# Edge attribute sums by sender: from a product over all blocks to pre-summed rows added in DRAM

## The chip, the cores and the metric

The kernel runs on one core of one Trainium2 chip. The metric is device time in microseconds (us) of one execution. Of the kernel before there are three runs, 2778.34, 2779.93 and 2783.31 us (median 2779.93), and one profiled execution.

## The reference

A graph of 3125 nodes (128 features) and 50000 edges, sorted by receiver `dst`, goes through four layers: a mean aggregation repeated three times, an MLP on edge means, an attention layer (GATv2) and a convolution with radial weights. What matters here is the second layer's input and the first layer beside which it is made:

```
# layer 1, three times: every node adds the mean of its senders' rows
neigh = segment_sum(h[src], dst) / max(deg, 1);  h = h + neigh
# layer 2: means of the 16 edge attributes, by sender and by receiver
rec_attr  = segment_sum(edge_attr_16, src) / max(count(src), 1)
sent_attr = segment_sum(edge_attr_16, dst) / max(count(dst), 1)
h = leaky_relu(concat([x, rec_attr, sent_attr]) @ W1 + b1) @ W2 + b2
```

The receivers are sorted, so edges of one receiver lie together. The senders are random.

## The kernel before

Nodes are padded to 3200, 25 blocks (NBLK) of 128. Edges come in 391 tiles of 128. A visit is a pair of a tile and a block of receivers that it touches: there are 415 visits (NV), taken in 83 batches (NB) of five (VB). An edge of a tile belongs to just one visit; in the others it counts as invalid.

After a setup (ids and attributes are gathered, turned by PE transposes and copied into the tiles EI and AT, the fills of L574 and L829), the adjacency matrix is built in PSUM and stored in DRAM (L849, L1307, L583, L391). Then comes the stage that the change touches.

**The aggregation stage.** It has 75 steps: three layers of 25 blocks of receivers. In a step PE multiplies the block's row of the adjacency (1.6 MB, 3200 columns by 128 partitions) with H, 25 f32 products that the profile counts as 50 (L1335). Three such rows fit into SBUF (RING = 3); SP fetches the row of step n from DRAM when step n-3 is done (L396, L397), 66 fetches in all. DVE scales the sums and adds them (`update_block`, L886 to L898).

Beside a step, one batch of edge attributes is summed; eight steps of the second layer have two (`BATCH_OF`, L196). DVE prepares a batch (`attr_batch`, L861):

- For the sums by receiver: one-hot rows OHD in bf16 (five compares, L881) and the attributes cut into three bf16 parts (L870, L875, L879, L883, L884), whose products are exact enough. PE multiplies 128x48 per visit into the block of receivers that a register names (L1322).
- For the sums by sender: since a sender can be in any of the 25 blocks, DVE makes the one-hot of the block (L871), the one-hot of the row in the block in f32 (`one_hot`, L836), and `products`, the attributes and a one (SA = 17 columns) times the block's one-hot, 25 x 17 = 425 columns per visit (L876). PE multiplies 128x425 in f32 into one bank, where all sums by sender grow (L1319).

DVE runs one step ahead: it prepares the batches of step n+1, then updates the block of step n. `attr_batch(k)` waits until PE has summed batch k-2 (L865), since buffers alternate. PE waits for `attrs_hot` (L1317) and, ahead of a step, for the block updated two steps before (L1332).

GpSimd (POOL) does nothing in this stage. In later stages it issues indirect DMAs, which gather 128 rows by a list of indices: L518 in the attention's scores, L535 in the convolution. After the stage DVE divides both sums (L909 to L916, to `means_ready`), PE turns the means, and the MLP follows.

Of the kernel before, what the change touches and what calls it, by code (L numbers as in the profile page):

```python
# [19 lines left out]
P = 128  # L20
# [6 lines left out]
VB = 5  # L27
# [38 lines left out]
SA = 17  # L66
# [9 lines left out]
def gnn_program(nc, x, edge_ids, last_dst, edge_attrs, species, w1a, w1b, b1, w2, row_params, wlr, wup,  # L76
                wr1, wr2, wdn_a, wdn_b, wsk, out):
    ctx = ExitStack()
    with ctx:
# [14 lines left out]
        radial_hidden = dram("radial_hidden", [VPG * RG * 8, P])  # L94
        dst_in_block = dram("dst_in_block", [VG * P * P], mybir.dt.int16)
# [11 lines left out]
        EI = sb("EI", [P, 5, VW])  # L107
# [115 lines left out]
        FILLS = [(g, j) for g in range(VG) for j in range(2)] + [(g, j) for g in range(VG) for j in range(2, 9)]  # L223
        N_FILL = len(FILLS)
        ACT_FILLS = 18
# [9 lines left out]
        def fill_copy(f):  # L235

            g, j = FILLS[f]
            n = 1 if j == 1 else 4
            if j < 2:
                w = P  # L240
                dst = view(EI, 4 * j * VW + g * P, [[VW, n], [1, w]])
            else:
                w = min(P, NV + 1 - g * P)
                row = (0, 4, 8, 12, SH, RAD, RAD + 4)[j - 2]
# [4 lines left out]
        def OHS(p):  # L249

            return view(OH, p * VB * P, [[P, VB], [1, P]])

        def products(p):

            return view(SCR, p * VB * NBLK * SA, [[NBLK * SA, VB], [SA, NBLK], [1, SA]])

        OHD_AT = 0
        PARTS3_AT = OHD_AT + 2 * VB * P // 2
        SBH_AT = PARTS3_AT + 2 * VB * 24
        LEFT_AT = SBH_AT + 2 * VB * NBLK  # L260
        assert LEFT_AT + 2 * VB * 16 <= DEPTH * VB * D
# [5 lines left out]
        def attr_parts(p):  # L267

            return view(G, PARTS3_AT + p * VB * 24, [[1, VB * 24]]).bitcast(BF16).rearrange("p (v n) -> p v n", v=VB)


# [22 lines left out]
        BACK = 5  # L294
# [78 lines left out]
        def _(sp):  # L373
# [6 lines left out]
            sp.dma_start(block_of_visit, vrow[:, 0:P]).then_inc(s("blocks_out"), 16)  # L380
            sp.wait_ge(s("blocks_out"), 16)
            sp.dma_start(rowi[:, 2 * NT:2 * NT + VW], block_of_visit.rearrange("g v -> (g v)").rearrange("(o n) -> o n", o=1)).then_inc(s("blocks_in"), 16)
            for g in range(VG):
                sp.wait_ge(s("kinds_ready"), g + 1)
                sp.dma_start(dst_in_block[g * P * P:(g + 1) * P * P].rearrange("(p n) -> p n", p=P),
                             view(RX, 20 * P + g * P // 2, [[1, P // 2]]).bitcast(mybir.dt.int16)).then_inc(s("near_stored"), 16)
                sp.wait_ge(s(f"attrs_in{g % 2}"), 16 * (g // 2 + 1))
                sp.dma_start(radial_rows[g * P:(g + 1) * P, :], view(SCR, (g % 2) * N_ATTR * P + 20 * P, [[1, 8 * P]])).then_inc(s(f"radial_rows_stored{g % 2}"), 16)
# [3 lines left out]
            for r in range(RING):  # L392
                sp.wait_ge(s(f"block_moved{r}"), 16 * len(range(r, NBLK, RING)))
            for n, (i, b, slot, fetch) in enumerate(STEPS):
                if fetch:
                    sp.wait_ge(s("block_summed"), n - RING + 1)  # L396
                    sp.dma_start(view(RX, slot * ABLK, [[1, ABLK]]), adjacency[b]).then_inc(s(f"block_moved{slot}"), 16)  # L397
            for i in range(2):
# [5 lines left out]
                if i == 0:  # L404
# [6 lines left out]
                    sp.wait_ge(s("radial_zeroed"), 1)  # L411
                    for j in range(VPG):
                        sp.dma_start(wr1_s[8 * j:8 * j + 8, 8 * j:8 * j + 8], wr1.rearrange("(a q) c -> a q c", q=VB)[:, 0, 0:8]).then_inc(s("radial_loaded"), 16)
                    for k in range(NB + DEPTH):
                        if k < NB:
                            if k >= DEPTH:
                                sp.wait_ge(s("z_hot"), k - DEPTH + 1)
                            sp.dma_start(near(k % DEPTH), dst_in_block[k * VB * P:(k + 1) * VB * P].partition_broadcast(P)).then_inc(s(f"near_in{k % DEPTH}"), 16)
                        if k >= DEPTH:
                            i, m = (k - DEPTH) % ROWS_RING, (k - DEPTH) // ROWS_RING  # L420
                            sp.wait_ge(s(f"score_gathered{i}"), 16 * VB * (m + 1))
                            sp.dma_start(gathered_rows[k - DEPTH], score_rows(i).rearrange("p a b -> p (a b)")).then_inc(s(f"rows_stored{i}"), 16)
# [31 lines left out]
        def _(pool):  # L454
# [23 lines left out]
            for g in range(VG):  # L478
                at = bass.IndirectOffsetOnAxis(ap=tvi[:, g:g + 1], axis=0)
                if g >= 2:  # L480
                    pool.wait_ge(s("fill_turned"), 2 * VG + 7 * (g - 1))
# [26 lines left out]
            pool.memset(wr1_s[:], 0.0).then_inc(s("radial_zeroed"), 1)  # L508
            pool.wait_ge(s("idx_made"), 1)
            pool.wait_ge(s("table_written"), written(1))  # L510
            for k in range(NB):
                i, m = k % ROWS_RING, k // ROWS_RING
                if k >= ROWS_RING:
                    pool.wait_ge(s("z_read"), k - ROWS_RING + 1)
                    pool.wait_ge(s(f"rows_stored{i}"), 16 * m)
# [26 lines left out]
        def _(act):  # L542
# [33 lines left out]
            act.wait_ge(s("near_stored"), 16 * VG)  # L576
# [55 lines left out]
            def weights_and_hot(k, p):  # L632
# [7 lines left out]
                for q in range(VB):  # L640
                    ins = act.activation(OH[:, p, q, :], iota[:], ACT.Abs, bias=view(EI, 3 * VW + VB * k + q, [[1, 1]]), scale=-1.0)
# [25 lines left out]
        def _(dve):  # L667
# [88 lines left out]
            dve.wait_ge(s("blocks_in"), 16)  # L756
# [41 lines left out]
            for g in range(VG):  # L798
# [4 lines left out]
                st = [view(RX, (5 * g + i) * P, [[1, P]]) for i in range(5)]  # L803
# [3 lines left out]
                done(dve.tensor_scalar(st[3], dr[:, 1], tv[:, 5, g:g + 1], None, ALU.add))  # L807
                va, vb, vc = (view(HT, 1792 + 128 * i, [[1, P]]) for i in range(3))
                dve.tensor_copy(view(RX, 20 * P + g * P // 2, [[1, P // 2]]).bitcast(mybir.dt.int16), st[3])
                dve.tensor_copy(st[2], view(HT, 1664, [[1, P]]).bitcast(I32))  # L810
                dve.tensor_copy(vc, view(HT, 1536, [[1, P]]).bitcast(I32))
                done(dve.tensor_scalar(va, st[3], 0.0, None, ALU.is_ge))
                done(dve.scalar_tensor_tensor(vb, st[3], float(P - 1), va, ALU.is_le, ALU.mult))

                done(dve.scalar_tensor_tensor(vc, vb, -64.0, vc, ALU.mult, ALU.add))
                dve.tensor_scalar(st[1], vc, 64.0, None, ALU.add)
                dve.tensor_scalar(invalid_neg[:, g, :], vb, 1.0, BIG, ALU.subtract, ALU.mult)
                done(dve.tensor_tensor(va, dr[:, 1], dr[:, 2], ALU.not_equal))
                dve.tensor_tensor(st[4], va, vb, ALU.mult).then_inc(s("kinds_ready"), 1)
# [3 lines left out]
            dve.wait_ge(s("fill_copied_act"), 2 * VG)  # L823
# [8 lines left out]
            dve.wait_ge(s("ones_made"), 2)  # L832
# [6 lines left out]
            dve.wait_ge(s("key_iota_made"), 2)  # L839
# [17 lines left out]
            dve.memset(PS[:, 2, :], 0.0)  # L857
            dve.memset(PS[:, 4:8, :], 0.0).then_inc(s("sums_zeroed"), 1)
            dve.wait_ge(s("visit_built"), NVA)

            def attr_batch(k):  # L861
# [4 lines left out]
                attrs = lambda n: view(AT, VB * k, [[1, VB], [NV + 1, n]])  # L866
                part = lambda j: attr_parts(p)[:, :, j * 16:(j + 1) * 16]
                left = view(G, LEFT_AT + p * VB * 16, [[16, VB], [1, 16]])
                sbh = lambda dims: view(G, SBH_AT + p * VB * NBLK, dims)
                dve.tensor_copy(part(0), attrs(16))  # L870
# [4 lines left out]
                split = mark(dve.tensor_tensor(left, attrs(16), part(0), ALU.subtract))  # L875
# [4 lines left out]
                for q in range(VB):  # L880
                    dve.tensor_scalar(OHD(p)[:, q], iota_h[:, KEYS:KEYS + P], view(EI, 3 * VW + VB * k + q, [[1, 1]]), None, ALU.is_equal)  # L881
                dve.wait_ge(s("dve_step"), split)
                done(dve.tensor_tensor(left, left, part(1), ALU.subtract))  # L883
                dve.tensor_copy(part(2), left).then_inc(s("attrs_hot"), 1)  # L884

# [15 lines left out]
            for n in range(LAYERS * NBLK):  # L901
# [3 lines left out]
                update_block(n)  # L905
            dve.wait_ge(s("attrs_summed"), NB)
            by_src = view(PS, 2 * 512, [[SA, NBLK], [1, SA]])
            by_dst = view(PS, 4 * 512, [[DSLOT, NBLK], [16, 3], [1, 16]])
            done(dve.tensor_scalar(small[:, 0, :], by_src[:, :, 16], 1.0, None, ALU.max))  # L909
            done(dve.reciprocal(inv_deg[:, 0, :], small[:, 0, :]))  # L910
            dve.tensor_copy(means[:, :, 0:16], by_src[:, :, 0:16])
            done(dve.tensor_copy(means[:, :, 16:32], by_dst[:, :, 0, :]))
            done(dve.tensor_tensor(means[:, :, 16:32], means[:, :, 16:32], by_dst[:, :, 1, :], ALU.add))
# [108 lines left out]
            for i in range(DEPTH, ROWS_RING):  # L1022
                dve.wait_ge(s(f"rows_stored{i}"), 16 * len(range(i, NB, ROWS_RING)))
# [539 lines left out]
```

## Time and profile before

| | |
|---|---|
| median of three runs | 2779.93 us |
| profiled execution | 2787.6 us |
| its span | 2785.8 us |
| PE busy | 2016.9 us (72%) |
| DVE busy | 2019.5 us (72%) |
| ACT busy | 499.4 us (18%) |
| POOL busy | 896.0 us (32%) |
| share of the chain that ended last | PE 40%, POOL 23%, DVE 21%, issue 12% |
| costliest lines of that chain | PE L1335 14%, PE L1319 9%, POOL L518 9% and 6%, POOL L535 8% |

The span is the profiled execution from its first to its last instruction; 1.8 us lie around it. Busy shares are means over stages with different limits: PE and DVE have the same 72%, and which of the two sets the pace must be read stage by stage. A matmul's duration in a group's mean is longer than the distance to the next one, since matmuls are pipelined.

### The profile page before, as it was taken

The numbers are of one execution on the slowest core, as the hardware profiler recorded it, in microseconds if no ns is written. First come the engines' busy times: TensorE is split into PE (matmuls) and PEld (weight loads), VectorE is DVE, ScalarE is ACT, GpSimd is POOL, SyncE is SP. The second block draws the span as 40 slices with busy tenths as digits, with TensorE's granted clock in tenths as the row PEclk, the third lists the DMA queues.
The fourth block names the chain that finished last, engine by engine and source line by source line (L and its number), as shares of the span: only waits on it lengthen the run. The fifth ranks groups of instructions, "written<-read, shape, count | busy, mean of one in ns | idle before, by whom it ended". The sixth has DMA issues, their size and how long they took to land.

```text
span 2785.8 us, 42113 instructions
## 1 busy us (share of the span) xinstructions
PE 2016.9 (72%) x10841; PEld 1503.3 (54%) x10841; DVE 2019.5 (72%) x5209; ACT 499.4 (18%) x1184; POOL 896.0 (32%) x888
## 2 busy tenths in 40 slices
PE   3777777999899999985444334326884778878887
PEld 2322224888678888854333333315773656666666
DVE  8888888778797777767555555578557777777775
ACT  2222221000000000011000000002221444444441
POOL 2000000000000000004777777725000577777770
PEclk9999999999999999997555555556896676777778
DMA  5222223453234344504444444413441222222120
GB/s 182 97 119 95 119 95 142 168 183 123 95 130 178 119 166 166 187 2 138 126 128 125 129 126 124 127 60 114 125 127 30 64 53 53 53 54 53 53 53 27
DMA packets 98876, 300.01 MB, mean 108 GB/s; under 512 B 21520, under 2 KB 48919, under 8 KB 86432
## 3 DMA queue, kind: packets, MB, share of 16 engines
q1 hardware_dynamic: 69566, 232.90, 24.6%
q0 software_dynamic: 27904, 64.15, 8.8%
q8 instruction: 100, 1.64, 0.2%
q10 hardware_dynamic: 1250, 0.86, 0.1%
q14 instruction: 56, 0.46, 0.1%
HBM read 220.86 MB, written 76.97 MB: 107 GB/s over the span
## 4 chain that ended last, share of the span: by engine, by line
PE 40%; POOL 23%; DVE 21%; issue 12%; DMA 2%; ACT 1%; SPq 1%; DVEq 0%; POOLq 0%; ACTq 0%
PE PS L1335 14%; PE PS L1319 9%; POOL G L518 9%; POOL G L535 8%; POOL SCR L518 6%; DVE SCR L849 5%; PE PS L1439 5%; DVE G L848 4%; PE PS L1474 3%; DVE SCR L876 2%; PE PS L1307 1%; PE PS L1462 1%; PE PS L1308 1%; PE PS L1442 1%; PE PS L1309 1%
## 5 line engine op out<-in xcount | busy, mean ns | idle before, releaser
L518 POOL DMA_INDIRECT G<-table,src_idx x255 | 259.7, 1019 | 1296.9 <-DMA table<-RX 1219.5
L535 POOL DMA_INDIRECT G<-table,gather_idx x415 | 415.5, 1001 | 373.7 <-DMA table<-RX 247.5
L1394 PE MATMUL PS<-RX,OH 128*128 x830 | 208.2, 434 | 310.4 <-DVE OH L964 309.7
L1474 PE MATMUL PS<-SCR,OH 128*128 128x256 f32 x830 | 309.8, 544 | 108.7 <-DVE SCR L1204 108.7
L1394 PEld LDWEIGHTS PS<-RX,OH 128*128 128x128 f32 x830 | 183.7, 322 | 338.6 <-issue 337.8
L876 DVE TENSOR_TENSOR SCR<-G,AT 128x2125 f32<-128x2125 f32 x83 | 318.9, 3842 | 0.0
L1319 PE MATMUL PS<-SCR,OH 128*128 128x425 f32 x830 | 312.7, 523 | 3.5 <-DVE G L884 3.2
L1474 PEld LDWEIGHTS PS<-SCR,OH 128*128 128x128 f32 x830 | 218.6, 273 | 168.7 <-DVE RX L1169 110.8
L1335 PE MATMUL PS<-HB,RX 128*128 128x132 f32 (+1 forms) x2500 | 292.5, 277 | 0.6 <-ACT RX L583 0.6
L1335 PEld LDWEIGHTS PS<-HB,RX 128*128 128x128 f32 x2500 | 283.9, 191 | 1.0 <-ACT RX L583 1.0
L849 DVE TENSOR_SCALAR SCR<-iota_h,OH 128x400 bf16<-128x400 int16 x790 | 250.4, 317 | 0.0
L848 DVE TENSOR_SCALAR G<-iota_h,OH 128x128 bf16<-128x128 int16 x790 | 195.9, 248 | 53.5 <-PE PS L1309 48.9
L1307 PE MATMUL PS<-SCR,G 128*128 128x400 bf16 x395 | 142.2, 360 | 103.7 <-DVE SCR L849 73.8
L1319 PEld LDWEIGHTS PS<-SCR,OH 128*128 128x128 f32 x830 | 151.6, 191 | 116.8 <-issue 112.5
L836 DVE TENSOR_TENSOR OH<-iota,EI 128x640 f32<-128x640 f32 x166 | 145.0, 874 | 76.8 <-PE PS L1442 76.7
L1439 PE MATMUL PS<-G,OH 128*128 128x128 f32 x830 | 162.4, 348 | 49.4 <-issue 25.9
L1169 DVE TENSOR_TENSOR RX<-RX,PS 128x256 f32 x415 | 171.1, 412 | 13.9 <-PE PS L1474 2.3
L518 POOL DMA_INDIRECT SCR<-table,src_idx x160 | 160.8, 1005 | 48.7 <-issue 48.7
L1439 PEld LDWEIGHTS PS<-G,OH 128*128 128x128 f32 x830 | 137.0, 223 | 65.0 <-issue 57.2
L1335 PE MATMUL PS<-SCR,RX 128*128 128x128 f32 x1250 | 148.1, 279 | 7.2 <-DVE SCR L896 7.2
L583 ACT COPY RX<-PS 128x400 f32<-128x400 f32 x200 | 98.5, 492 | 284.4 <-PE PS L1309 283.8
L1185 DVE TENSOR_TENSOR SCR<-G,AT 128x480 f32<-128x480 f32 x83 | 54.7, 659 | 130.7 <-DMA G<-table,gather_idx 84.3
(309 smaller groups left out, 2904.6 us busy)
## 6 DMA issues: line engine op xcount, KB each, us to landing
RX<-adjacency SPq DMA_DIRECT2D x66, 1600.0 KB, 6.7
adjacency<-RX SPq DMA_DIRECT2D x25, 1600.0 KB, 6.1
RX<-gathered_rows SPq DMA_DIRECT2D x83, 320.0 KB, 3.0
gathered_rows<-G SPq DMA_DIRECT2D x51, 320.0 KB, 2.4
AT<-dst_in_block SPq DMA_DIRECT2D x83, 160.0 KB, 3.9
gathered_rows<-SCR SPq DMA_DIRECT2D x32, 320.0 KB, 2.4
G<-table,gather_idx POOLq DMA_INDIRECT x415
G<-table,src_idx POOLq DMA_INDIRECT x255, 2.7
```

Of the source, the lines that this page charges most:

```text
L518: pool.indirect_dma_start(score_rows(i)[:, q], None, tables[0], bass.IndirectOffsetOnAxis(ap=src_idx[:, v:v + 1], axis=0)).then_inc(s(f"sc ...
L535: pool.indirect_dma_start(G[:, p, q, :], None, tables[i], bass.IndirectOffsetOnAxis(ap=gather_idx[:, p, q:q + 1], axis=0)).then_inc(s(f"{n ...
L848: dve.tensor_scalar(src_hot(v, j), iota_h[:, KEYS:KEYS + P], KS[:, 2 + j, v:v + 1], None, ALU.is_equal)
L849: ins = dve.tensor_scalar(key_hot(v, j), iota_h[:, 0:KEYS], KS[:, j, v:v + 1], None, ALU.is_equal)
L876: dve.tensor_tensor(products(p), sbh([[NBLK, VB], [1, NBLK], [0, SA]]), view(AT, VB * k, [[1, VB], [0, NBLK], [NV + 1, SA]]), ALU.mult)
L1169: dve.tensor_tensor(acc, acc, PS[:, q, 0:MSG], ALU.add).then_inc(s("added"), 1)
L1307: pe.matmul(PSF[:, bass.ds(bank, KEYS)], src_hot(v, 0), key_hot(v, 0), start=False, stop=False, skip_group_check=True)
L1319: pe.matmul(PS[:, 2, 0:NBLK * SA], OHS(p)[:, q], products(p)[:, q], start=False, stop=False, skip_group_check=True)
L1335: ins = pe.matmul(PS[:, n % 2, 0:w], adj(slot)[:, c], H_OF[i][:, c, 0:w], start=c == 0, stop=c == NBLK - 1)
L1394: ins = pe.matmul(view(PS, k % DEPTH * 1024 + 171 * q, [[1, XR_W]]), view(OH, (k % DEPTH * VB + q) * P, [[1, P]]), view(RX, b * XR_W, [[1, ...
L1439: pe.matmul(PSF[:, bass.ds(b * P, P)], OH[:, p, q, :], G[:, p, q, :], start=False, stop=False, skip_group_check=True)
L1474: ins = pe.matmul(PS[:, q, 0:MSG], OH[:, p, q, :], view(SCR, M_AT + (p * VB + q) * MSG, [[1, MSG]]), start=True, stop=True)
```

## The change

Sums by sender are no longer made by one product over all blocks. For each visit PE multiplies a 128x128 matrix of 0 and 1, which says which edges of the tile have the same sender, with the attributes in bf16 parts. Every edge then holds the sum over its twins, the edges of the visit with its sender. The first of each set of twins is found, and its row of 49 values (three parts of 16 and the count) is added to the sender's row of a DRAM table by an indirect DMA that accumulates. There are five tables, one for each place q of a visit in its batch; an add to a table waits until the table's last add has landed. The other edges send their rows to 128 spare rows.

- Setup: 24 fills instead of 36 (the radial attributes' rows and one kind are no longer turned). The sender's key is stored to DRAM too as int16 rows (`sender_of_visit`). SP clears the five tables (five DMAs of 3328 x 49 values).
- `attr_batch`: L871, L836 and L876 go. Five compares (`twin_hot`) between the keys of all 128 edges in a row, fetched by SP as a broadcast DMA of 160 KB per batch (`row16_in`), and the edge's own key come.
- PE: five bf16 products of 128x51 (48 attribute parts, a one, and two columns that mark whether an earlier edge has the same sender) take the place of L1319.
- `place`, new on DVE after `update_block`: it copies the five sums from PSUM, compares the two marks with limits made of the partition number, and writes the row to which each edge's sum goes.
- POOL: 83 x 5 indirect DMAs that add.
- After the last step SP reads the five tables back, DVE adds them, and the means use the three parts.

```diff
 def attr_batch(k):
...
-    split = mark(dve.tensor_tensor(sbh([[NBLK, VB], [1, NBLK]]), view(iota, 0, [[0, VB], [1, NBLK]]),
-                                   view(EI, VW + VB * k, [[1, VB], [0, NBLK]]), ALU.is_equal))
-    one_hot(OHS(p), 2, k)
+    dve.wait_ge(s(f"row16_in{k % DEPTH}"), 16 * (k // DEPTH + 1))
+    for q in range(VB):
+        dve.tensor_scalar(twin_hot(p)[:, q], sender(k % DEPTH)[:, q * P:(q + 1) * P], EI[:, 1, VB * k + q:VB * k + q + 1], None, ALU.is_equal)
...
-    dve.tensor_tensor(products(p), sbh([[NBLK, VB], [1, NBLK], [0, SA]]),
-                      view(AT, VB * k, [[1, VB], [0, NBLK], [NV + 1, SA]]), ALU.mult)
...
+def place(k):
+    sums = twin_sums(k % DEPTH)
+    both = view(begins, FLAG_AT, [[2, VB], [1, 2]])
+    first = view(begins, FLAG_AT + 2 * VB, [[1, VB]])
+    dve.wait_ge(s("twins_summed"), k + 1)
+    if k >= DEPTH:
+        for q in range(TABLES):
+            dve.wait_ge(s(f"scattered{q}"), 16 * (k - DEPTH + 1))
+    dve.tensor_copy(sums, view(PS, (2 + k % 2) * 512, [[TWIN_W, VB], [1, TWIN_W]])).then_inc(s("twins_copied"), 1)
+    dve.wait_ge(s("twins_copied"), k + 1)
+    done(dve.tensor_tensor(both, sums[:, :, SENT_W:TWIN_W], limits, ALU.is_lt))
+    done(dve.tensor_tensor(first, both[:, :, 0], both[:, :, 1], ALU.mult))
+    done(dve.tensor_tensor(first, first, key_shift[:, VB * k:VB * (k + 1)], ALU.mult))
+    dve.tensor_scalar(sent_to[k % DEPTH], first, dummy, None, ALU.add).then_inc(s("sent_placed"), 1)
...
 # PE, attr_sums(k)
+    if k >= 2:
+        pe.wait_ge(s("twins_copied"), k - 1)
     for q in range(VB):
-        pe.matmul(PS[:, 2, 0:NBLK * SA], OHS(p)[:, q], products(p)[:, q], start=False, stop=False, skip_group_check=True)
+        ins = pe.matmul(PS[:, 2 + p, q * TWIN_W:(q + 1) * TWIN_W], twin_hot(p)[:, q], attr_parts(p)[:, q, 0:TWIN_W], start=True, stop=True)
+    ins.then_inc(s("twins_summed"), 1)
...
 # POOL
+pool.wait_ge(s("sent_cleared"), 16 * TABLES)
+for k in range(NB):
+    pool.wait_ge(s("sent_placed"), k + 1)
+    for q in range(VB):
+        if k >= 1:
+            pool.wait_ge(s(f"scattered{q}"), 16 * k)
+        pool.indirect_dma_start(sent_sums[q], bass.IndirectOffsetOnAxis(ap=sent_to[k % DEPTH][:, q:q + 1], axis=0),
+                                twin_sums(k % DEPTH)[:, q, 0:SENT_W], None, compute_op=ALU.add).then_inc(s(f"scattered{q}"), 16)
...
 # SP, in the loop over steps, and after it
+    for k in BATCH_OF[n]:
+        if k >= DEPTH:
+            sp.wait_ge(s("attrs_hot"), k - DEPTH + 1)
+        sp.dma_start(sender(k % DEPTH), sender_of_visit[k * VB * P:(k + 1) * VB * P].partition_broadcast(P)).then_inc(s(f"row16_in{k % DEPTH}"), 16)
...
+sp.wait_ge(s("block_summed"), LAYERS * NBLK)
+for q in range(TABLES):
+    sp.wait_ge(s(f"scattered{q}"), 16 * NB)
+    sp.dma_start(sent(q), sent_sums[q][0:NPAD, :].rearrange("(p n) d -> p (n d)", p=P)).then_inc(s("sent_in"), 16)
...
 # DVE, ahead of the means
+dve.wait_ge(s("sent_in"), 16 * TABLES)
+for q in range(1, TABLES):
+    done(dve.tensor_tensor(sent(0), sent(0), sent(q), ALU.add))
```

## Rows read from the trace of the kernel before

**Rows 1.** Busy time in 500:600 us: busy us (count) by engine; clock, DMA share, GB/s
```profile
500.00:600.00 100.00, 100.00 (x688) 80.74 (x687) 78.18 (x193) 0.00 (x0) 0.00 (x0) 1.00 0.51 181
```

**Rows 2.** Groups in 460:1211 us: line, engine, operation; busy us, mean ns; idle, releaser
```profile
L1319 PE MATMUL PS<-SCR,OH 128*128 128x425 f32 x830 | 312.7, 523 | 3.5 <-DVE G L884 3.2
...
L876 DVE TENSOR_TENSOR SCR<-G,AT 128x2125 f32<-128x2125 f32 x83 | 318.9, 3842 | 0.0
...
L836 DVE TENSOR_TENSOR OH<-iota,EI 128x640 f32<-128x640 f32 x83 | 67.9, 818 | 0.0
...
L881 DVE TENSOR_SCALAR G<-iota_h,EI 128x128 bf16<-128x128 int16 x415 | 74.7, 252 | 0.0
...
L870 DVE CAST G<-AT 128x80 bf16<-128x80 f32 x83 | 19.6, 236 | 142.8 <-PE PS L1322 142.8
```

**Rows 3.** One step in order of time: start us, length us, engine, line, operation, count
```profile
503.12 5.87 PE L1335 MATMUL PS<-HB,RX 128*128 128x132 f32 x50
...
503.31 0.24 DVE L870 CAST G<-AT 128x80 bf16<-128x80 f32 x1 [1.82 <-PE PS L1322]
...
508.83 3.74 PE L1319 MATMUL PS<-SCR,OH 128*128 128x425 f32 x10
...
509.74 0.15 DVE L892 TENSOR_SCALAR small<-PS 128x1 f32<-128x1 f32 x1
...
510.57 0.29 DVE L898 SCALAR_TENSOR_TENSOR X<-SCR,X 128x128 f32<-128x128 f32 x1
...
512.40 0.29 PE L1322 MATMUL PS<-G 128*128 128x48 bf16 x5
...
512.53 5.87 PE L1335 MATMUL PS<-HB,RX 128*128 128x132 f32 x50
```

**Rows 4.** The stage's first matmuls, its first wide product, and its end, in order of time
```profile
460.32 5.89 PE L1335 MATMUL PS<-HB,RX 128*128 128x132 f32 x50 [0.58 <-ACT RX L583]
...
469.39 5.53 PE L1319 MATMUL PS<-SCR,OH 128*128 128x425 f32 x10 [3.18 <-DVE G L884]
...
1210.63 0.18 DVE L909 TENSOR_SCALAR small<-PS 128x25 f32<-128x25 f32 x1 [3.02 <-PE PS L1322]
...
1214.11 0.57 DVE L916 TENSOR_TENSOR means<-means,inv_deg 128x400 f32<-128x400 f32 x1
```

**Rows 5.** Groups of the whole span: a PSUM read and a long add on DVE
```profile
L1169 DVE TENSOR_TENSOR RX<-RX,PS 128x256 f32 x415 | 171.1, 412 | 13.9 <-PE PS L1474 2.3 <-DVE RX L1169 0.7
...
L952 DVE TENSOR_TENSOR HB<-RX 128x3200 f32<-128x3200 f32 x1 | 3.5, 3493 | 0.2 <-ACT RX L601 0.2
```

**Rows 6.** Gathers on POOL and a compare on DVE, in order of time
```profile
1398.71 0.95 POOL L518 DMA_INDIRECT G<-table,src_idx  x1 [0.30 <-issue]
...
1398.96 0.54 DVE L964 TENSOR_SCALAR OH<-AT,tv 128x640 f32<-128x640 int16 x1
...
1405.20 0.96 POOL L518 DMA_INDIRECT G<-table,src_idx  x1 [0.30 <-issue]
```

**Rows 7.** Busy time in 2250:2350 us, columns as in Rows 1
```profile
2250.00:2350.00 100.00, 82.70 (x315) 63.52 (x314) 74.25 (x185) 46.40 (x122) 76.57 (x77) 0.73 0.20 53
```

**Rows 8.** DMA issues: KB each, us to landing; last, queue in 500:600 us: packets, MB, share
```profile
RX<-adjacency SPq DMA_DIRECT2D x66, 1600.0 KB, 6.7
...
AT<-dst_in_block SPq DMA_DIRECT2D x83, 160.0 KB, 3.9
...
SCR<-table,src_idx POOLq DMA_INDIRECT x160, 2.7
...
radial_rows<-SCR SPq DMA_DIRECT2D x4, 512.0 KB, 2.7
...
SCR<-in_edge_attrs,tvi POOLq DMA_INDIRECT x4, 9.4
...
q1 hardware_dynamic: 1584, 18.02, 50.5%
```

**Rows 9.** One operation of the setup's loop over groups, in order of time
```profile
43.57 0.29 DVE L815 SCALAR_TENSOR_TENSOR RX<-RX 128x128 f32<-128x128 f32 x1
```

More of the change, by code:

```diff
@@ L94, in gnn_program @@
         radial_hidden = dram("radial_hidden", [VPG * RG * 8, P])
+        sender_of_visit = dram("sender_of_visit", [VG * P * P], mybir.dt.int16)
+        sent_sums = [dram(f"sent_sums{q}", [NPAD + P, SENT_W]) for q in range(TABLES)]
         dst_in_block = dram("dst_in_block", [VG * P * P], mybir.dt.int16)
@@ L237, in fill_copy, with sender, twin_hot, twin_sums @@
             g, j = FILLS[f]
-            n = 1 if j == 1 else 4
-            if j < 2:
+            n = 4
+            if j == 0:
                 w = P
-                dst = view(EI, 4 * j * VW + g * P, [[VW, n], [1, w]])
+                dst = view(EI, g * P, [[VW, n], [1, w]])
             else:
                 w = min(P, NV + 1 - g * P)
-                row = (0, 4, 8, 12, SH, RAD, RAD + 4)[j - 2]
+                row = (0, 4, 8, 12, SH)[j - 1]
                 dst = view(AT, row * (NV + 1) + g * P, [[NV + 1, n], [1, w]])
             return dst, view(PS, (2 + f % 6) * 512, [[P, n], [1, w]])
[L249 to L255, printed above, removed]
         OHD_AT = 0
[L258 to L261, printed above, removed]
+        EQ_AT = DEPTH * VB * P // 2
+        TWINS_AT = EQ_AT + 2 * VB * P // 2
+        LEFT_AT = TWINS_AT + 2 * VB * 26
+        FLAG_AT = LEFT_AT + 2 * VB * 16
+        assert FLAG_AT + 3 * VB <= 4 * NT + 600
+        SUMS_AT = RAD * (NV + 1)
+        SENT_AT = SUMS_AT + DEPTH * VB * TWIN_W
+        SHIFT_AT = SENT_AT + DEPTH * VB
+        LIMIT_AT = SHIFT_AT + NV + 1
+        assert LIMIT_AT + 16 <= ROWS * (NV + 1) and VB * TWIN_W <= 512
+        ZERO_AT = ROWS * (NV + 1) - (NBLK + 1) * SENT_W
+        assert LIMIT_AT + 16 <= ZERO_AT
+        def sender(i):
+            return view(begins, i * VB * P // 2, [[1, VB * P // 2]]).bitcast(mybir.dt.int16)
+        def twin_hot(p):
+            return view(begins, EQ_AT + p * VB * P // 2, [[1, VB * P // 2]]).bitcast(BF16).rearrange("p (v n) -> p v n", v=VB)
+        def twin_sums(i):
+            return view(AT, SUMS_AT + i * VB * TWIN_W, [[TWIN_W, VB], [1, TWIN_W]])
+        sent_to = [view(AT, SENT_AT + i * VB, [[1, VB]]).bitcast(I32) for i in range(DEPTH)]
+        key_shift = view(AT, SHIFT_AT, [[1, NV]])
+        limits = view(AT, LIMIT_AT, [[0, VB], [1, 2]])
+        marks = view(AT, LIMIT_AT + 2, [[0, VB], [1, 3]])
+        dummy = view(AT, LIMIT_AT + 5, [[1, 1]])
         def OHD(p):
@@ L806, in _ @@
                 dve.tensor_scalar(view(HT, 1664, [[1, P]]).bitcast(I32), idr[:, 0:P], 127, None, ALU.bitwise_and)
[L807 to L810, printed above, removed]
+                done(dve.tensor_scalar(st[2], dr[:, 1], tv[:, 5, g:g + 1], None, ALU.add))
@@ L811, in _ @@
+                va, vb, vc, vd = (view(HT, 1792 + 128 * i, [[1, P]]) for i in range(4))
+                row16 = lambda at: view(RX, at + g * P // 2, [[1, P // 2]]).bitcast(mybir.dt.int16)
+                dve.tensor_copy(row16(20 * P), st[2])
+                dve.tensor_copy(vd, view(HT, 1664, [[1, P]]).bitcast(I32))
                 dve.tensor_copy(vc, view(HT, 1536, [[1, P]]).bitcast(I32))
-                done(dve.tensor_scalar(va, st[3], 0.0, None, ALU.is_ge))
-                done(dve.scalar_tensor_tensor(vb, st[3], float(P - 1), va, ALU.is_le, ALU.mult))
@@ L815, in _ @@
-                done(dve.scalar_tensor_tensor(vc, vb, -64.0, vc, ALU.mult, ALU.add))
-                dve.tensor_scalar(st[1], vc, 64.0, None, ALU.add)
+                done(dve.tensor_scalar(va, st[2], 0.0, None, ALU.is_ge))
+                done(dve.scalar_tensor_tensor(vb, st[2], float(P - 1), va, ALU.is_le, ALU.mult))
                 dve.tensor_scalar(invalid_neg[:, g, :], vb, 1.0, BIG, ALU.subtract, ALU.mult)
+                done(dve.scalar_tensor_tensor(vc, vd, float(NBLK), vc, ALU.mult, ALU.add))
@@ L818, in _ @@
+                done(dve.scalar_tensor_tensor(vc, iota[:], -1.0, vc, ALU.mult, ALU.add))
+                done(dve.scalar_tensor_tensor(vc, vc, -float(NPAD), vb, ALU.add, ALU.mult))
+                done(dve.scalar_tensor_tensor(st[1], vc, float(NPAD), iota[:], ALU.add, ALU.add))
+                dve.tensor_copy(row16(22 * P), st[1])
                 done(dve.tensor_tensor(va, dr[:, 1], dr[:, 2], ALU.not_equal))
-                dve.tensor_tensor(st[4], va, vb, ALU.mult).then_inc(s("kinds_ready"), 1)
+                dve.tensor_tensor(st[3], va, vb, ALU.mult).then_inc(s("kinds_ready"), 1)
```

139 lines of the change are left out of this document (84 added, 55 removed).

## The prediction

> **What bounds the kernel now.** I read the page first: its table of engines and its costliest groups name two lines of the aggregation stage, L1319 and L876. Then the busy time by stretches. In 500 to 600 us TensorE (PE) is busy 100.00 of 100 us at granted clock 1.00 (2.4 GHz), VectorE (DVE) 78, GpSimd (POOL) none, and the DMA engines 0.51 of the time [rows 1]. The reader is to see that one engine has no slack, one has a fifth, and one sleeps. The groups of the stage say what PE and DVE do: the wide product of L1319 takes 312.7 us of PE, L876 prepares it in 318.9 us of DVE, and DVE's only large wait, 142.8 us at L870, is for PE [rows 2]. Last the order of one step: 50 adjacency matmuls start at 503.12, the wide product at 508.83, the short product L1322 at 512.40, the next step's at 512.53. A period is 9.41 us: 5.71 + 3.57 + 0.13 [rows 3]. The stage runs from 460.32 to the means at 1214.68 (1214.11 + 0.57), 754.4 us [rows 4]. It is PE's, step after step.
>
> **What goes.** PE's 3.57 us per batch. On DVE: L876, 3.84 us per batch, L836 at 0.82 and the little L871. A batch of DVE work now spans 503.31 to 509.74, 6.43 us, of which the three hold about 4.7 (3.84 + 0.82; L871 overlaps mostly), so some 1.8 stay.
>
> **What comes on PE.** Five bf16 products of 51 columns per batch. The nearest row is L1322, five of 48 columns in 0.29 us. So PE needs 5.71 + 0.13 + 0.29 = 6.13 us for a step with one batch. The wait on twins_copied is for the batch two back, done long before.
>
> **What comes on DVE.** Five compares for the twins, like L881's (five take 0.9 us: 74.7 us for 83 batches [rows 2]): a batch is 2.7 us. The block update is 1.12 us at most (509.74 to 510.57 + 0.29). place() copies 128x255 from PSUM, nearest L1169 with 0.41 [rows 5], and has four tiny operations that wait on each other; such a one takes some 0.2 with its wait in the update's chain: 1.3 in all. Sum 2.7 + 1.1 + 1.3 = 5.1 us, under 6.13. In the eight steps with two batches it is 8.7 at the lower update cost, above PE's 6.6. Wait added: place() waits for this step's twin product, and behind it stands the next attr_batch; the product follows block_summed by 0.3 us while the update runs, so it costs nothing as long as PE is not late. It also waits for the scatters of batch k-3, which matters only if POOL lags.
>
> **What comes on POOL.** This sets the end, I think. There are 5 x 83 = 415 indirect DMAs that add rows in DRAM, on an engine that is idle here. The trace has no scatter and no add. The nearest rows are POOL's gathers of 128 rows: 0.95 us busy, and five of them with their gaps take 1398.71 to 1405.20 = 6.49 us, 1.30 each [rows 6]. Another stage runs at the same pace, 77 in 100 us [rows 7]. 6.49 per batch is already above PE's 6.13 and DVE's 5.1: POOL becomes the bound, and in steps with two batches (13.0) even more; POOL falls back there until place() holds DVE, DVE holds PE. So the stage is 83 times POOL's pace, x.
>
> What could x be? Lower end: 0.96 each, without the 0.30 between (issue gaps stand ahead of all gathers, so I don't believe it); then PE and DVE bind: 67 x 6.13 + 8 x 8.7 = 480 us. Nearest row: 6.49. Upper end: POOL may not add to table q before the add of the batch before has landed. A gather lands 2.7 us after issue, one of 14 KB rows 9.4 [rows 8]. If each add took 9.4 and the round did not start earlier, x would be about 10. Between them are the DMA engines. In 500 to 600 us ten fetches and a bit moved 18.02 MB in 1584 packets, 11.4 KB each, at 50.5% of the engines' time [rows 8]: 4.8 us a fetch. A scatter gives each of 16 engines eight rows, and a row may have to wait for such a packet, about 0.5 us (50.5 us x 16 / 1584). Eight times that on 2.7 is 6.8 us, just over the 6.49 after which POOL comes back to the same table, and a stall results only in rounds that meet a fetch. I take x = 7.0: the row plus 0.5 for an add that is dearer than a gather and for these stalls. It is nearer to 6.49 than to 10 because everything measured of POOL's small indirect DMAs is in the low row.
>
> On the same point the Trainium skill, "SBUF — State Buffer", section "SBUF: two separate sides", speaks against the change: while VectorE runs an instruction in a mode with two ports, GpSimd cannot write descriptors and waits for the end. Each batch would have ten compares on DVE. Whether it holds is seen at L964, a tensor_scalar from int16 of 128x640 in 0.54 us, shorter than L836 of the same size (0.82): it began 0.25 us into a gather, and the gather still took 0.95 [rows 2, 6]. The trace does not bear the rule out here, though that is one kind of compare with a float output. Its price is a rival below.
>
> **The other ends.** Lead: the first batch was ready at 469.39 [rows 4]. DVE now has some 3 us of constants ahead and 3.8 us less in the batch, then batch 1 (2.7), update and place: first scatter about 474, so 13.7 us after 460.3. Tail, all exposed, since PE and DVE have nothing else: the last add lands 1.4 after its issue ends (2.7 less about 1.3), the last table of 612 KB comes in 3.0 (512 KB took 2.7 [rows 8]), four dependent adds of 1225 columns at 3.49 / 3200 us a column [rows 5] are 5.7 with gaps, the means chain 4.1 as now and one more operation 0.6: 14.8 us. Setup: three more dependent operations of 0.33 (0.29 like L815 [rows 9], and its wait) and a copy in each of four groups, against 12 fewer fills and one transposed kind less: +2 us, between -3 and +5. The five clears (3.1 MB) lie in the setup beside DVE's work; each scatter table waits for them, 400 us later. Sender rows, 160 KB each: such a DMA lands in 3.9 us [rows 8], issued two steps ahead, 13 us. Fetches land in 6.7, also with two steps' lead: at a step of 7 they stay hidden; doubled they would not. SP's order is no trouble: sender k waits only for attrs_hot of k-3.
>
> **Sum.** After: 13.7 + 83 x + 14.8 + 2 = 30.5 + 83 x, against 754.4. With x = 7.0: 611.5, a gain of 142.9. The profiled execution took 2787.6 us (its span 2785.8, 1.8 around it), so 2644.7 by its scale; the median of the runs is 2779.93, 7.7 below, so **2637 us**. Other stages are left as they are: their instructions don't change, and what is queued behind the scatters on POOL, the score gathers of L518, waits for a table that is written only after the MLP.
>
> **The rivals.**
> - Cheap scatters: PE and DVE bind. 9 + 480 + 1.3 + 5 + 14.8 + 2 = 512: 2538 us. For it: nothing but the 0.96 of busy time; against it the 0.30 ahead of each gather. Chance 0.05.
> - The DMA engines are the bound. Per batch 4.8 (fetch) + 0.6 (sender row, estimate: a tenth of a fetch's bytes in shorter rows) + scatters. A gather costs an engine 0.20 x 100 / 77 = 0.26 us [rows 7]; an add must read twice and write: twice that, five times, is 2.6. Sum 8.0, x = 8.0: 694.5, gain 59.9, 2720 us. For it: shares of one engine set do add up. Against: nine of 75 steps have no fetch, and the fetch's 4.8 was taken with nobody else there. Chance 0.17. A fall of PE's clock belongs here: at 0.73, as in [rows 7], 5.71 becomes 7.8 and a step 8.2, 75 of them 618 us: 2675, inside the forecast's own range. That row, where PE is busy 83 of 100 us, speaks for such a fall, since PE would be busy 6.1 of 7.0 us here.
> - DVE's compares lock POOL out: ten at 0.165 is 1.65 a batch, x = 8.14: 706, 2731 us. Against it stands L964. Chance 0.08. (The rule is the one of the page named above.)
> - Slower than before: POOL's wait for its own table. If an add needs 10 us from issue to semaphore, each of the five tables admits one add per 10 us: x = 10, 860.5 us, 106 more than now, 2886 us. It decides from x = (754.4 - 30.5) / 83 = 8.72. For it: the reads and writes in DRAM beside 1.6 MB fetches and the 9.4 us row. Against: 2.7 us for every small gather, among 320 KB stores. Chance 0.14.
> - No change: PE's product is gone but the pace of scatters falls on 8.65 to 8.79. Chance 0.03.
>
> **Numbers.** The forecast (x from 6.49 to 7.8, that is 2595 to 2703) has 0.53. Faster by over 0.2%, which is what a measurement of this kernel can tell: 0.53 + 0.05 + 0.17 + 0.08 = 0.83; within: 0.03; slower: 0.14. The range leaves out the slower case and the cheapest: 2580 to 2755.
>
> **What would show it.** Right: in the profile after, POOL is busy over 70% from about 474 to 1055 and its gaps at the scatter name mostly issue; PE waits for DVE, DVE for POOL's scatters, in the steps after the first double ones; PE's product is 0.29 us; the tail from last scatter to means is 15 us. Wrong: POOL idle before each scatter for the DMA of its table (latency), a scatter busy for clearly more than 0.96 us (descriptors or DVE's lock), fetches landing after 13 us (DMA engines), or a granted clock under 0.9 in the stage.

## The result: 3% slower, and the profile after

The changed kernel takes 2865.98 us (median of four runs, 2863.96 to 2870.28) against 2781.6 us of the kernel before beside it: ratio 1.0305, interval 1.0289 to 1.0321. The forecast was 2637 us. The profiled execution has a span of 2862.8 us, 77.0 more than before.

The busy times by stretch come first, as in [rows 1] (window; PE, weight load, DVE, ACT, POOL busy; granted clock, DMA share, GB/s):

```profile
500.00:600.00 100.00, 77.47 (x673) 73.93 (x671) 47.10 (x254) 0.00 (x0) 78.08 (x52) 0.89 0.86 216
600.00:700.00 100.00, 72.39 (x587) 68.89 (x585) 50.86 (x272) 0.00 (x0) 80.74 (x52) 0.80 0.69 148
700.00:800.00 100.00, 59.56 (x434) 53.51 (x432) 45.27 (x242) 0.00 (x0) 83.15 (x54) 0.73 0.57 110
```

PE had 100 of 100 us at clock 1.00 and now idles; DVE fell from 78 to 47; POOL, idle before, is the busiest. But it does only 52 to 54 scatters in 100 us, where the gathers of [rows 7] came to 77. The line of the scatter says why (durations in ns, minimum / median / maximum; then what POOL waited for, in us and times; then who waited for it):

```profile
L554 POOL DMA_INDIRECT sent_sums<-AT x415: 1552/1553/1804, 478.7 to 1278.8; - x139
its engine sat idle before it (us, times) until:
  DVE AT L968: 411.6, 1
  issue: 110.4, 361
  DMA sent_sums<-AT: 45.6, 53
who waited for it (us, times):
  DVE AT L963: 398.3, 62
```

An indirect DMA that adds keeps POOL busy for 1.55 us; a gather took 0.95 [rows 6]. The 411.6 us are the time before the first one. From 478.7 to the end of the last at 1280.4 there are 801.7 us: 645.7 busy, 110.4 of the gap ahead of each, 45.6 of waits for a table's DMA. That is 9.66 us a batch (7.78 + 1.33 + 0.55). DVE waits 398 us for scatters in place(), and PE waits for DVE behind it. One step in order of time, the rows that answer to [rows 3]:

```profile
883.88 5.82 PE L1427 MATMUL PS<-SCR,RX 128*128 128x128 f32 x50
884.43 1.55 POOL L554 DMA_INDIRECT sent_sums<-AT  x1 [0.30 <-issue]
886.29 1.55 POOL L554 DMA_INDIRECT sent_sums<-AT  x1 [0.30 <-issue]
...
890.00 1.55 POOL L554 DMA_INDIRECT sent_sums<-AT  x1 [0.30 <-issue]
...
891.73 0.43 DVE L963 COPY AT<-PS 128x255 f32<-128x255 f32 x1 [9.06 <-DMA sent_sums<-AT]
...
895.60 0.40 PE L1410 MATMUL PS<-begins 128*128 128x51 bf16 x5 [5.89 <-DVE begins L952]
...
895.82 1.55 PE L1414 MATMUL PS<-begins,G 128*128 128x48 bf16 x5
...
897.27 3.11 PE L1427 MATMUL PS<-SCR,RX 128*128 128x128 f32 x13
```

The adjacency matmuls take 5.8 us as before. Then DVE has waited 9.06 us for the scatters of the batch three back, prepares the next batch late, and PE stands 5.89 us until it is ready. POOL issues every 1.86 us all through this step.

The rest went as the change intended. The groups of the stage answer to [rows 2]: the twin product is cheap, and no DVE group is above 80 us where L876 had 319.

```profile
L1410 PE MATMUL PS<-begins 128*128 128x51 bf16 x415 | 27.5, 199 | 176.0 <-DVE begins L952 124.1 <-DVE AT L963 51.6 <-issue 0.2
```

```profile
L941 DVE TENSOR_SCALAR begins<-begins,EI 128x128 bf16<-128x128 int16 x415 | 78.7, 292 | 4.0 <-DMA begins<-sender_of_visit 4.0
```

The end of the stage, as in [rows 4] (from the last scatter to the means, start and length in us):

```profile
1278.83 1.56 POOL L554 DMA_INDIRECT sent_sums<-AT  x1 [0.30 <-issue]
1289.69 5.85 DVE L995 TENSOR_TENSOR RX<-RX 128x1225 f32<-128x1225 f32 x4 [33.99 <-DMA RX<-sent_sums]
...
1299.54 0.58 DVE L1006 TENSOR_TENSOR means<-means,inv_deg 128x400 f32<-128x400 f32 x1
```

The stage, from the first adjacency matmul (462.0) to the means (1300.1), takes 838.1 us instead of 754.4. It costs 83.7; setup adds 1.7, and 8.4 come back after the means. These 8.4 are not the change's doing: in this execution POOL's 830 gathers are about 0.01 us shorter each (8.9 us in sum), and in the changed kernel's second profile, where they have their old length, what follows the means takes 1570.9 us, as before (1571.1).

### The profile page after: what moved, and what is told of

Its sections match the earlier page's. It is cut to its first block, busy times and chain, and to the rows that moved or that the text cites. A ratio compares the mean times of both kernels' runs of the same rounds, so it can differ in the third digit from the quotient of the medians.

```text
span 2862.8 us, 42728 instructions
## 1 busy us (share of the span) xinstructions
PE 1843.6 (64%) x10390; PEld 1453.3 (51%) x10390; DVE 1802.7 (63%) x5818; ACT 494.8 (17%) x1175; POOL 1533.1 (54%) x1303
## 3 DMA queue, kind: packets, MB, share of 16 engines
q0 software_dynamic: 87664, 74.59, 15.0%
## 4 chain that ended last, share of the span: by engine, by line
POOL 34%; PE 18%; DVE 17%; issue 15%; DMA 14%; ACT 1%; DVEq 0%; POOLq 0%; ACTq 0%
DMA sent_sums<-AT 12%; POOL sent_sums L554 12%; POOL G L565 9%; POOL G L582 7%; POOL SCR L565 6%; PE PS L1531 5%; DVE SCR L900 5%; DVE G L899 4%; PE PS L1566 3%; PE PS L1396 1%; PE PS L1554 1%; PE PS L1397 1%; PE PS L1398 1%; DVE RX L1259 1%; PE PS L1534 1%
## 5 line engine op out<-in xcount | busy, mean ns | idle before, releaser
L554 POOL DMA_INDIRECT sent_sums<-AT x415 | 645.7, 1556 | 567.6 <-DVE AT L968 411.6
L565 POOL DMA_INDIRECT G<-table,src_idx x255 | 257.1, 1008 | 165.0 <-DMA table<-RX 87.6
L1427 PE MATMUL PS<-HB,RX 128*128 128x132 f32 (+1 forms) x2500 | 326.1, 296 | 6.6 <-DVE HB L980 6.0
L1427 PEld LDWEIGHTS PS<-HB,RX 128*128 128x128 f32 x2500 | 317.8, 210 | 7.4 <-DVE HB L980 6.1
L1566 PEld LDWEIGHTS PS<-SCR,OH 128*128 128x128 f32 x830 | 216.7, 271 | 159.9 <-DVE RX L1259 100.4
L963 DVE COPY AT<-PS 128x255 f32<-128x255 f32 x83 | 35.2, 424 | 398.6 <-DMA sent_sums<-AT 398.3
L1259 DVE TENSOR_TENSOR RX<-RX,PS 128x256 f32 x415 | 171.6, 414 | 14.8 <-PE PS L1566 3.6
L1427 PE MATMUL PS<-SCR,RX 128*128 128x128 f32 x1250 | 174.7, 309 | 9.4 <-DVE SCR L980 9.4
L1427 PEld LDWEIGHTS PS<-SCR,RX 128*128 128x128 f32 x1250 | 170.6, 224 | 9.6 <-DVE SCR L980 9.5
L1531 PEld LDWEIGHTS PS<-G,OH 128*128 128x128 f32 x830 | 142.8, 238 | 61.4 <-issue 54.7
L1554 PEld LDWEIGHTS PS<-wr_s,SCR 40*128 40x128 f32 x830 | 128.4, 236 | 48.0 <-issue 48.0
L1554 PE MATMUL PS<-wr_s,SCR 40*128 40x128 f32 x830 | 146.5, 334 | 6.3 <-DMA SCR<-radial_hidden 4.5
```

The costliest lines, as they stand in the source:

```text
L554: pool.indirect_dma_start(sent_sums[q], bass.IndirectOffsetOnAxis(ap=sent_to[k % DEPTH][:, q:q + 1], axis=0), twin_sums(k % DEPTH)[:, q, 0 ...
L565: pool.indirect_dma_start(score_rows(i)[:, q], None, tables[0], bass.IndirectOffsetOnAxis(ap=src_idx[:, v:v + 1], axis=0)).then_inc(s(f"sc ...
L1259: dve.tensor_tensor(acc, acc, PS[:, q, 0:MSG], ALU.add).then_inc(s("added"), 1)
L1427: ins = pe.matmul(PS[:, n % 2, 0:w], adj(slot)[:, c], H_OF[i][:, c, 0:w], start=c == 0, stop=c == NBLK - 1)
L1531: pe.matmul(PSF[:, bass.ds(b * P, P)], OH[:, p, q, :], G[:, p, q, :], start=False, stop=False, skip_group_check=True)
L1554: ins = pe.matmul(view(PS, 5 * 512 + q * P, [[1, P]]), view(SCR, CH_AT + p * P, [[1, P]], 8 * VB), wr2_s[:, q, :], start=True, stop=True)
```

## The experiments

Theory A: the addition is what lengthens POOL's instruction, and 415 of them set the pace. Rivals: B, it is the direction (a scatter, whose indices choose rows in DRAM to be written); C, it is the wait of an add for its own table that sets the pace; D, POOL's time goes by the rows or bytes of an instruction. "Stage" is always from the first adjacency matmul to the means, in the profile. The first run of each of the first four experiments was on one chip, without the changed kernel beside them, so their times are compared with the kernel before alone; the length of an instruction is read from their profiles.

**Writing instead of adding.** On that chip the kernel before took 3031 us; it was run again on another.

```diff
-    twin_sums(k % DEPTH)[:, q, 0:SENT_W], None, compute_op=ALU.add)
+    twin_sums(k % DEPTH)[:, q, 0:SENT_W], None)
```

> The scatters write their rows instead of adding them (the addition is left out, so the tables hold only the last write). Theory A, the addition is what makes POOL's instruction 1.55 us instead of a gather's 0.95: each scatter is busy about 0.95 us, 1.26 with its gap, the pace is 6.3 to 6.5 us a batch, 3.2 us less than the 9.66 measured, and the time falls by 83 x 3.2 = 260 us to about 2600. Theory B, the direction costs (indices on the DRAM side, whatever is done there): 1.55 us stays and the time stays at 2866 within 10 us. Theory C, the wait for the own table sets the pace (landing): busy falls or not, but POOL's idle for the table's DMA takes the place, over 3 us a batch, and the time stays above 2800.

> As the first of its kind (rows written, not added; the sums by sender are wrong for it), for the pace: there POOL's scatter was busy 0.97 us, yet the pace was 8.6 us a batch, with PE starved of instructions (idle before it named issue, 217 us). Theory A, that was the chip: here PE has no such idle and the pace is 6.5 us, time about 2600. Rival, plain scatters starve PE's instruction supply anywhere, or the fetch collides with them: PE idle stays, pace over 8, time over 2730.

First run: 3003.8 us, ratio 0.990 (0.987 to 0.994), with 216.9 us of PE's idle ahead of L1427 named issue, that is, waiting for nothing that the profile shows. Its cause is open; it is absent in the second run, and the pace is read from that one. Second: 2696.16 us, 0.9665 (0.964 to 0.969), stage 657.1 us. The line of the scatter in the second:

```profile
L554 POOL DMA_INDIRECT sent_sums<-AT x415: 963/969/1177, 480.6 to 1099.4; - x139
its engine sat idle before it (us, times) until:
  DVE AT L968: 416.8, 11
  DMA sent_sums<-AT: 114.9, 95
```

In both, 0.97 us instead of 1.55: the addition is what lengthens the instruction, and B falls. The same kernel with nothing but the addition taken out is 6.8 points faster on the ratio than the changed kernel beside it (1.0342, below). What POOL does in the extra 0.58 us no run shows. But the pace is 7.5 us a batch (619.8 / 83: 4.87 busy, 1.17 of gaps, 1.38 for tables), not the 6.5 expected. The rival C has a part: as POOL gets round sooner, it meets tables whose last write hasn't landed, 114.9 us in 95 waits, where it was 45.6 in 53.

**No scatters.** POOL's loop, and the waits for it in place() and on SP, are taken out.

> No scatter is issued at all and nobody waits for one (the sums by sender are left out; tables are cleared and read back as in the changed kernel). It is the floor of PE and DVE. Theory A, POOL's 415 instructions alone set the pace: my sum for PE and DVE, 67 x 6.13 + 8 x 8.7 = 480 us for the steps, so the stage ends at about 462 + 9 + 480 + 13 = 964 instead of 1300, 336 us earlier, time about 2530. Rival, the adjacency fetches (9.0 us to landing in the changed kernel) or the sender rows set a pace of their own at 7.5 to 8 us a step: 2600 to 2640 with PE waiting for DMA. Rival, PE's clock falls as in the changed kernel (0.8) although nothing waits: about 2600.

> No scatters at all (the sums by sender are left out), now beside a kernel before of usual time. The stage alone took 506 us to the means on the other chip; so here 2785 - 754 + 510 = about 2540, with PE at granted clock 1.00 and no idle in it. If the other chip's other stages had hidden something, 2600 or more.

On the first chip 2755.73 us, 0.909 (0.906 to 0.911); on the second 2543.76 us, 0.9115 (0.910 to 0.913), stage 506.1 us:

```profile
500.00:600.00 100.00, 100.00 (x1008) 99.74 (x1007) 76.22 (x417) 0.00 (x0) 0.00 (x0) 1.00 0.84 302
```

PE is full at clock 1.00, with 1008 matmuls in 100 us where it had 688 [rows 1]: 60 a step, so 6.0 us. In the steps with two batches (600 to 700 us) it was 87 of 100. Fetches land in 7.2 us, and PE waits for them 5.6 us in all. The stage was expected at 502 us (9 + 480 + 13), so the floor of PE and DVE is where I had put it, and without scatters the fetches and the clock are no bound of their own. What lies between 506 and 838 us comes with the scatters.

**Half the rows.**

```diff
-    ap=sent_to[k % DEPTH][:, q:q + 1] ... twin_sums(k % DEPTH)[:, q, 0:SENT_W]
+    ap=sent_to[k % DEPTH][0:64, q:q + 1] ... twin_sums(k % DEPTH)[0:64, q, 0:SENT_W]
```

> Each scatter adds 64 rows instead of 128 (the edges in the upper 64 places of each tile are left out of the sums by sender). If POOL's time goes by descriptors, 1.55 us becomes something like 0.9 to 1.1 and the time falls by 415 x 0.5 = about 200 us to 2660. If it is a fixed cost of an adding instruction, 1.55 stays and the time stays at 2866 less the table waits (at most 45 us of idle).

3050.97 us on the slower chip, 1.007 (1.003 to 1.011).

```profile
L554 POOL DMA_INDIRECT sent_sums<-AT x415: 1413/1419/1644, 481.5 to 1244.7; - x139
```

64 rows cost 1.42 us, 128 cost 1.55. By these two, 0.13 us goes with 64 rows; drawn on in a straight line (an estimate), about 1.28 us is left for an instruction without rows. So most of it is paid by instruction.

**Narrow rows.** 17 values instead of 49, in other tables.

```diff
-    pool.indirect_dma_start(sent_sums[q], ... twin_sums(k % DEPTH)[:, q, 0:SENT_W]
+    pool.indirect_dma_start(sent_narrow[q], ... twin_sums(k % DEPTH)[:, q, 0:SEND_W]
```

> Each added row has 17 values (68 B) instead of 49 (196 B), in tables of their own that nobody reads (the sums by sender come out as zero). If bytes count for POOL's 1.55 us or for the DMA engines, the busy time or the waits for the table shrink, and fetches land earlier than 9.0 us: up to 45 us less. If only the number of rows counts, nothing moves: 1.55 us, 2866 within 15 us.

3093.46 us on that chip, 1.020 (1.017 to 1.023); the scatter 1552 ns at the median, the table waits 47.6 us. Bytes count for nothing in POOL's time, and rows for 0.13 us in 64: D falls. The number of packets stayed as it was (87664 in the software queue), so this run doesn't say what fewer packets would do.

**Fewer scatters.** If it is paid by instruction, some visits are better off on PE. The last one, or the last two, of the five visits of a batch go by the old wide product, which needs the sender's block and row again (made from the ids by six DVE operations ahead of the loop), two one-hots and the product on DVE in each batch, and shares PSUM bank 7.

```diff
+WIDE = 2                     # 1 in the other
+TABLES = VB - WIDE
...
+    dve.tensor_tensor(products(p), sbh([[NBLK, WIDE], [1, NBLK], [0, SA]]),
+                      view(AT, VB * k + TABLES, [[1, WIDE], [0, NBLK], [NV + 1, SA]]), ALU.mult)
...
+    for q in range(WIDE):
+        pe.matmul(PS[:, 7, 64:64 + NBLK * SA], OHS(p)[:, q], products(p)[:, q], start=False, stop=False, skip_group_check=True)
```

> The changed kernel itself, beside the others on this chip, since the first four experiments ran on a chip where the kernel before took 3031 us instead of 2780. All theories: 3% over the kernel before on a chip with its usual time; POOL's scatter 1.55 us. If the ratio here is far from 1.03, the ratios of the first four can't be put against it.

> Four of five visits of a batch go by scatter, the fifth by the old wide product (two f32 matmuls of 425 columns, DVE prepares 1 x 425). If POOL's 1.86 us for each scatter is the pace, 4 x 1.86 = 7.44 us a batch plus the table waits 0.4: 83 x 7.8 = 650 + 31 = 681 against 754 of the kernel before: 2705. If it isn't the count of scatters but their latency in the table's chain (one a round, whatever the number), the pace stays at 9.66: 2865.

> Three of five visits by scatter, two by the wide product. POOL: 3 x 1.86 = 5.6 us a batch. PE: 5.84 + 0.13 + 0.17 + 2 x 0.71 = 7.5 us; DVE 5.1 - 0.35 + 2 x 0.97 = 6.7. PE is the bound again: 67 x 7.5 + 8 x 12.5 = 603 + 25 = 628 against 754: about 2655. If the table's chain of latency were the pace: 2865, and if DVE is (with the waits for its own results longer than counted), 2700.

> The same kernel as before with three tables, beside the one with six on the same chip: 0.972 of the kernel before, within 0.003.

The changed kernel again: 2884.03 us, 1.0342 (1.0325 to 1.0359). With four scatters 2801.07, 1.0048 (1.0031 to 1.0065), stage 761.7. With three 2712.5, 0.9717 (0.9701 to 0.9733), and in a second call 2714.22, 0.9721 (0.9703 to 0.9738); stage 673.6. So the time does fall with the count, but one scatter less took the stage from 845.9 us (the changed kernel beside it) to 761.7, 84 us where 157 were expected, and two less fell short too (2655 expected). The line with three scatters shows the table waits, which I had counted at 0.4 us a batch, at 1.7:

```profile
L569 POOL DMA_INDIRECT sent_sums<-AT x249: 1551/1553/3122, 484.1 to 1121.1; - x125
its engine sat idle before it (us, times) until:
  DVE AT L996: 435.9, 24
  DMA sent_sums<-AT: 143.7, 66
...
DMA to landing us min/median/max: 3.1/6.3/10.0
```

This is the only kernel so far whose profile gives the landing of an add: 6.3 us at the median, up to 10.0, against 2.7 of a gather [rows 8]. A round of three scatters would be 5.6 us, less than that, so POOL often meets a table whose last add is under way. The waits for it grow as the rounds shrink: 45.6, 105.0, 143.7 us for five, four, three scatters a batch.

The same line shows a second cost, one that the wide product brings in: the median is still 1553 ns, but the longest add took 3122. The mean is 1711 with three scatters and 1613 with four, against 1556 with five. In order of time:

```profile
505.13 1.62 DVE L970 TENSOR_TENSOR SCR<-G,AT 128x850 f32<-128x850 f32 x1
505.14 3.12 POOL L569 DMA_INDIRECT sent_sums<-AT  x1 [0.30 <-issue]
```

L970 makes `products` from two inputs in SBUF. The add that began 0.01 us after it ended 1.51 us behind the product's end (508.26 and 506.75), about as long as a whole add. In this run 67 of the 249 adds began while L970 ran, and every one ended 1.43 to 1.51 us after the product did, however much of it was left: the add gets on only when the product is over. Over 1.55 us each, that is 36 us of POOL's busy time. How much of it was on the path no run separates.

**Six tables.** Odd and even batches add to different tables.

```diff
+    t = q + k % 2 * TABLES
+    if k >= 2:
+        pool.wait_ge(s(f"scattered{t}"), 16 * (k // 2))
```

> The kernel with three visits by scatter and two by the wide product, but with six tables instead of three: odd and even batches have tables of their own, so an add waits for the one two batches back. There POOL stood idle 143.7 us for a table's DMA, whose landing took 3.1 to 10.0 us (median 6.3). Theory: that idle is on the path in part, PE then sets the pace at about 7.5 us in single steps; less 40 to 60 us, plus 6 to 8 us for three more tables to read and add: 2660 to 2680. Rival: the idle was slack beside PE's pace and nothing is gained, 2715 to 2720. Rival: three adds more in flight delay the adjacency's fetches and one another, slower than 2712.

2677.55 us, 0.9594 (0.9581 to 0.9608), stage about 641 us (639.7 from the first matmul in the profile, which lacks the records of some ahead of it), and the fastest of all that compute the whole result: 4% under the kernel before, 7% under the changed one. It is 36.7 us below the same kernel with three tables beside it, so theory C's share is shown too, at this length of round.

```profile
L570 POOL DMA_INDIRECT sent_sums<-AT x249: 1551/1662/3109, 485.1 to 1079.4; - x125
its engine sat idle before it (us, times) until:
  DVE AT L997: 524.7, 62
  issue: 56.4, 185
  DMA sent_sums<-AT: 0.6, 2
```

The table waits are gone (0.6 us). POOL now waits for DVE (524.7 less the first 416.4). In 500 to 600 us PE was busy 100.00 with three tables already; what the second set gave lies later. The stretch 800 to 900 us, three tables and then six:

```profile
800.00:900.00 100.00, 89.92 (x708) 78.10 (x707) 64.80 (x262) 0.00 (x0) 58.83 (x35) 0.95 0.82 217
800.00:900.00 100.00, 100.00 (x840) 89.18 (x839) 80.92 (x323) 0.00 (x0) 75.59 (x44) 1.00 0.80 206
```

The adds that begin beside the wide product are still long (mean of all 1729 ns).

## Why the prediction was wrong

- **What bounds the kernel before: right.** Without scatters the stage took 506 us; my sum for cheap scatters gave 512, of which 2 are setup and 6.3 the last scatters and their landing, which this run doesn't have. PE 6.0 us a step (6.13 forecast). That floor is also the measure of the gain that there was to take.
- **POOL becomes the bound, DVE waits in place(), PE behind it: right**, and in the order named.
- **The failed step: "I take x = 7.0: the row plus 0.5 for an add that is dearer than a gather and for these stalls".** The row of the gather (6.49) was taken for an instruction that adds. It measured 7.78 + 1.33 + 0.55 = 9.66 (busy, gaps, table waits). The addition in POOL's busy time is 5 x 0.6 = 3.0 us more than five gathers' 4.75; the gaps and waits were 1.88 where 7.0 had left them 2.25, which makes the 2.66 us too few. 83 x 2.66 = 221 of the stage's error of 229 us (838.1 against 13.7 + 581 + 14.8 = 609.5); lead and tail are the other 8. I had the number of instructions, the engine and the chain right, and gave the one operation that no row showed 0.5 us a batch over a gather's row, at most 1.3 at the range's end of 7.8, when nothing but its likeness to a gather held it there.
- **The rivals.** The slower case (chance 0.14) had nearly the size (x = 10, 2886 us), and its mechanism wrong, so its nearness is luck: it named the landing of an add, and POOL stood only 45.6 us for a table. Landing is real, 6.3 us at the median with three tables, but it is mostly hidden while a round of five lasts 9.3 us. An instruction longer than a gather was named only among the signs, and had no rival and no chance of its own.
- **DMA engines as the bound: no.** Their share rose to 0.86 in 500 to 600 us and fetches landed in 9.0 us instead of 6.7. Yet L1427 never waited for a fetch, and POOL waited for a table's DMA 45.6 of 801.7 us.
- **DVE locking POOL out: hardly by compares, but by products of two inputs.** Only 7 of 415 scatters took over 1.6 us, the longest 1.80, and with five compares from 701.90 to 703.10 the one from 702.04 took 1.55. The Trainium skill's rule ("SBUF — State Buffer", section "SBUF: two separate sides") has whichever starts first hold the shared port for its whole instruction, and the loser wait in full; beside the compares it may be DVE that waits. Their means are 292, 289 and 306 ns beside scatters and 247 to 248 without any; the median of L941 is 249 and its longest 586, so a few are stretched. It is off the path.
- **My test of that rule was no test.** L964 began after the gather, so by the rule it was not the gather that had to wait. The five gathers of [rows 6] held a better case. The longest of them began 0.32 us before the end of a product of two SBUF inputs (L993) and ended 0.83 us after it:

```profile
1403.26 0.81 DVE L993 TENSOR_TENSOR SCR<-SCR,rows_s 128x640 f32<-128x640 f32 x1
1403.75 1.15 POOL L518 DMA_INDIRECT G<-table,src_idx  x1 [0.30 <-issue]
```

  The changed kernel has no long product beside its scatters and hardly paid for this; the kernels with four and three scatters brought part of the product back, and did.
- **Lead, tail, setup.** 16.7 instead of 13.7 us (the first compares waited 3.97 us for the first sender row, which SP sends only after the adjacency is stored); 19.7 instead of 14.8 (from the end of the last scatter to the last table landed 9.3 us, 4.4 forecast: SP could ask for that table only 7.1 us after the add's start, where a gather's landing had given 2.7); setup 1.7 instead of 2.
- **The clock** fell to 0.73 to 0.89 with PE's idle, as I feared it might. The matmuls of a step after a long wait took 8.1 us instead of 5.8 in places. POOL set the pace, so I think that it cost little of itself; no run separates it.

## What to carry to other kernels

In these runs an indirect DMA costs the engine that issues it mostly by instruction, and by kind: gather 0.95, write 0.97, add 1.55 us. When a change moves work to a kind of it that the trace doesn't have, its busy time is the first thing to bound widely, and to measure by itself. Work taken off a full engine is best moved only as far as the receiving one keeps up: five scatters a batch lost 3%, three won 3%, and with a second set of tables 4%. A chain through a table in DRAM stays hidden only as far as the round is longer than a landing (9.3 us against 6.3 at the median); each shorter round brought more of it up. And the length of an instruction on POOL is to be read beside what DVE runs when it starts.

## What the runs showed of the hardware

- An adding indirect DMA keeps POOL busy 1.55 us for 128 rows and 1.42 for 64; a writing one 0.97, a gather 0.95. Row length (68 or 196 B) doesn't count.
- An add that begins while DVE runs a product of two SBUF inputs (128x850) ends 1.43 to 1.51 us after the product's end, 67 times of 67, up to 3.12 us in all. In the kernel before 65 gathers (1290 to 1760 us) began while L993 ran; every one ended 0.81 to 0.84 us after it, the longest with 1.52 us in all.
- The software queue moved 27904 packets in the kernel before, 87664 after, 41184 with writes and 61104 with half the rows. Less those of before, that is 144, 32 and 80 packets per scatter. The counts fit an add that sends each row as a packet of its own and 16 more; a write sends 128 rows in 32. The two lines are the changed kernel's and that of the second run with writes:

```profile
q0 software_dynamic: 87664, 74.59, 15.0%
```

```profile
q0 software_dynamic: 41184, 74.59, 10.6%
```

- An add in DRAM landed after 3.1 to 10.0 us (median 6.3) beside 1.6 MB fetches with three tables, and after 3.1 to 9.6 (median 4.1) with six; the fetches themselves went from 6.7 to 9.0 us in the changed kernel.
